# Two-layer transformer kernel: blank rows written earlier, a new order in the dense expert stage, and gate products moved from VectorE to GpSimd

## The reference, cut to what matters

```python
x = ln(x + attn0(x))          # attn0 ends in its own MLP: x1 + gelu(ln(x1) @ w1) @ w2
logits = einsum('bld,ed->ble', x, gate_weight)
kth_val = sort(logits.reshape(-1))[T * 6 - 1]        # one global threshold
gates = logits * (logits >= kth_val)
h = gelu(einsum('bld,ehd->bleh', x, w1) + b1)        # 8 experts, hidden 512
y = einsum('bleh,edh->blde', h, w2) + b2
x = ln(x + einsum('blde,ble->bld', y, gates))
x = ln(x + attn1(x)); x = ln(x + top2_moe(x))        # layer 1
```

## Time and profile before

| | |
|---|---|
| median of 3 runs | 1162.04 us (1162.0 to 1164.67) |
| profiled execution | 1153.58 us |
| its span | 1151.9 us |
| attention_0 | about 0 to 248 us |
| dense_0 | about 248 to 742 us |
| layer 1 | the rest |
| PE, DVE, ACT, POOL busy | 962.3, 863.6, 741.1, 406.5 us |
| granted TensorE clock, mean | 0.922 |

### The profile page before, as it was taken

One profiled execution on the slowest core, in us unless ns is written; L12 is line 12 of the kernel. 1 busy time (PEld: TensorE's weight loads), 2 busy tenths in 40 slices (PEclk: granted clock), 3 DMA queues, 4 the chain that ended last, 5 costly groups with the idle time before them and its releaser, 6 DMA issues. The chain is left out here.

```text
span 1151.9 us, 29135 instructions
## 1 busy us (share of the span) xinstructions
PE 962.3 (84%) x10214; PEld 611.6 (53%) x10214; DVE 863.6 (75%) x2339; ACT 741.1 (64%) x1409; POOL 406.5 (35%) x572
## 2 busy tenths in 40 slices
PE   3999999946788999949889999589888861899995
PEld 2788887733444444414334444256565541689852
DVE  2899898836569999549899877558999864688833
ACT  2666666637688888828676788346555530688834
POOL 3455455434443000000100100113676677366643
PEclk9999999978799999979999999769989875899998
DMA  4000000010002999863222110100111101233244
GB/s 128 4 3 3 4 3 3 4 58 0 1 19 74 174 170 166 163 164 97 75 86 87 55 49 17 57 22 28 32 47 48 46 23 48 77 88 83 76 108 131
DMA packets 87997, 72.61 MB, mean 63 GB/s; under 512 B 8994, under 2 KB 73764, under 8 KB 87856
## 3 DMA queue, kind: packets, MB, share of 16 engines
q1 hardware_dynamic: 79088, 60.05, 23.1%
q0 software_dynamic: 4544, 8.60, 2.3%
q10 hardware_dynamic: 4224, 2.10, 0.7%
HBM read 40.14 MB, written 31.49 MB: 62 GB/s over the span
## 5 line engine op out<-in xcount | busy, mean ns | idle before, releaser
L778 ACT ACTIVATE d__hf<-d__HB,d__d 128x512 f32<-128x512 f32 x288 | 185.8, 681 | 76.2 <-PE d__HB L1001 72.1
L839 DVE TENSOR_TENSOR d__hl<-d__hf,d__hh 128x1024 f16<-128x1024 f32 x144 | 175.6, 1224 | 30.8 <-ACT d__hh L783 28.7
L783 ACT ACTIVATE d__hh<-d__hf 128x1024 f16<-128x1024 f32 x144 | 152.2, 1057 | 4.6
L751 POOL TENSOR_SCALAR d__rstd<-d__mv 128x4 f32<-128x4 f32 x16 | 15.0, 937 | 383.8 <-DVE d__mv L953 383.8
L999 PE MATMUL d__YB<-d__hh,d__w2h 128*128 128x512 f16 x288 | 110.3, 383 | 30.7 <-DVE d__hl L839 30.7
L999 PE MATMUL d__HB<-d__xh,d__w1h 128*128 128x512 f16 x288 | 114.2, 396 | 0.0
L1000 PE MATMUL d__HB<-d__xl,d__w1h 128*128 128x512 f16 x288 | 114.1, 396 | 0.0
L1001 PE MATMUL d__HB<-d__xh,d__w1l 128*128 128x512 f16 x288 | 113.1, 393 | 0.0
L1001 PE MATMUL d__YB<-d__hh,d__w2l 128*128 128x512 f16 x288 | 110.4, 383 | 0.0
L1000 PE MATMUL d__YB<-d__hl,d__w2h 128*128 128x512 f16 x288 | 110.3, 383 | 0.0
L298 POOL TENSOR_SCALAR_AFFINE_SELECT a__pt<-a__pt 128x512 f32<-128x512 f32 x128 | 81.6, 661 | 71.7 <-ACT a__pt L341 71.5
(11 more groups left out here) (376 smaller groups left out, 2532.9 us busy)
## 6 DMA issues: line engine op xcount, KB each, us to landing
rows<-d__blank SPq DMA_DIRECT2D x72, 268.0 KB, 7.6
d__G<-gates SPq DMA_DIRECT2D x64, 256.0 KB, 3.1
c__xin<-rows SPq DMA_DIRECT2D x39, 134.0 KB, 2.2
d__stage<-e_w SPq DMA_DIRECT2D x16, 256.0 KB, 3.2
b__stage<-e_w SPq DMA_DIRECT2D x32, 128.0 KB, 2.2
c__yb<-parts SPq DMA_DIRECT2D x8, 256.0 KB, 8.3
c__yb<-parts ACTq DMA_DIRECT2D x8, 256.0 KB, 8.8
out<-c__xo SPq DMA_DIRECT2D x8, 256.0 KB, 2.3
```

The lines of the kernel that those rows point to most:

```text
L778: act.activation(hf[:, q, f], HB[:, f], gelu, scale=1.0 / WS, bias=b1[:, at:at + 1]).then_inc(s_["h_free"], 1)
L783: act.activation(hh[:, q, f - 1:f + 1], hf[:, q, f - 1:f + 1], ACT.Copy).then_inc(s_["hi_done"], 1)
L839: dve.tensor_tensor(hl[:, q, f], hf[:, q, f], hh[:, q, f], ALU.subtract).then_inc(s_["lo%d_done" % i], 1)
```

## The change

- The 72 blank DMAs move from `dense_0` to `attention_0`'s SP queue, behind its loads, five at a time, each five behind a further `hn_done` of attention's 16 steps. GpSimd fills the source, now four rows wide (128x536), once at the start; SP waits for the last of them at the stage's end.
- In `dense_0` DVE's loop over s is written in a new order: `hn` of chunk s+3 stands at the head of a step (ahead of `low(s, 1)`), the statistics of chunk s+4 stand ahead of `xa`, and the first weight split and `b2s` come later.
- The 22 raw results are folded at steps 31, 32, 34, 36, 38, 40, 41, 43, ... 68 (9 steps for 5), not one per step up to 52. `acc` has 8 chunks, not 4. The chunks end at steps 41, 44, 49, 57, 59, 65, 69 and 73.
- A raw result is multiplied by its gate row by GpSimd, in place; DVE only adds it (or copies it, where it opens a chunk). A `G` buffer is given back by the engine that used it.

The core of the diff, without declarations:

```diff
@@ attention_0, SP @@
+            sp.wait_ge(blank_set, 1)
+            for i in range(BLANKS * NC_):
+                if i % 5 == 0:
+                    sp.wait_ge(hn_done, i // 5 + 1)
+                sp.dma_start(blanks[:, i], blank[:]).then_inc(blanked, 16)
+            sp.wait_ge(blanked, 16 * BLANKS * NC_)
@@ raw_pair @@
-    i = s - FOLD_0
-    return M_JOBS + i if i >= 0 and kept_raw(M_JOBS + i) else None
+    for j in range(M_JOBS, FOLD_0):
+        if kept_raw(j) and FOLD_0 + (j - M_JOBS) * 9 // 5 == s:
+            return j
+    return None
@@ dense_0, SP @@
-            for i in range(BLANKS * NC_):
-                if i % 4 == 0:
-                    sp.wait_ge(s_["counted"], min(i // 4 + 1, ROUNDS + 2))
-                sp.dma_start(blanks[:, i], blank[:].to_broadcast([P, 4, ROW])).then_inc(s_["blanked"], 16)
...
-                wait(sp, s_["g_used"], k - G_RING + 1)
+                wait(sp, s_["g_out%d" % (k % G_RING)], k // G_RING)
@@ dense_0, GpSimd, after the rstd work of step s @@
+                if raw_pair(s) is not None:
+                    j = raw_pair(s)
+                    k = place[j]
+                    pool.wait_ge(s_["g_in%d" % (k % G_RING)], 16 * (k // G_RING + 1))
+                    pool.wait_ge(s_["yf%d" % (j % 2)], j // 2 + 1)
+                    pool.tensor_tensor(raw(j), raw(j), G[:, k % G_RING], ALU.mult).then_inc(s_["gated"], 1)
+                    pool.wait_ge(s_["gated"], j - M_JOBS + 1)
+                    pool.sem_inc(s_["g_out%d" % (k % G_RING)], 1)
@@ dense_0, fold @@
                 if kept_raw(j):
-                    ins = dve.tensor_tensor(to, raw(j), G[:, k % G_RING], ALU.mult)
+                    dve.wait_ge(s_["gated"], j - M_JOBS + 1)
+                    part = raw(j)
+                    if j in opens:
+                        sums.link(dve.tensor_copy(to, part))
...
                 if j not in opens:
-                    ins = dve.tensor_tensor(acc[:, c % 4], acc[:, c % 4], tmp[:], ALU.add)
+                    ins = dve.tensor_tensor(acc[:, c], acc[:, c], part, ALU.add)
```

More of the change, by code:

```diff
@@ L169, in parts_0, with attention_0 @@
                     step(what, s - stage, k)
-def attention_0(nc, d, keep):
+def attention_0(nc, d, keep, rows):
     with ExitStack() as ctx:
@@ L184, in attention_0 @@
         bo = m.sb("bo", [P, P])
+        blank = m.sb("blank", [P, 4, ROW])
+        blanks = rows.rearrange("(i p r) c -> p i r c", p=P, r=4)
+        blank_set, blanked = m.sem("blank_set"), m.sem("blanked")
         x = m.sb("x", [P, NT, C])
@@ L277, in _ @@
             pool.wait_ge(cleared, 4)
+            pool.memset(blank[:], BLANK).then_inc(blank_set, 1)
             pool.wait_ge(loaded, 16 * LOADS)
@@ L923, in _ @@
                         dve.wait_ge(s_["pb_free"], left[("logits", c)] + 1)
+                c = s + 3
+                if 0 <= c < M_JOBS:
+                    if c:
+                        right_full(dve, "lift", c - 1)
+                    dve.wait_ge(s_["rstd0_done"], c + 1)
+                    for a in range(4):
+                        ins = dve.tensor_scalar(hn[:, a, :], x1[:, 4 * c + a, :], mv0[:, a, 0:1], rstd0[:, a:a + 1],
+                                                ALU.subtract, ALU.mult)
+                        ins.then_inc(s_["hn_done"], 1) if a == 3 else first.inc(ins)
                 if 0 <= s < JOBS:
@@ L943, in _ @@
                     left_full(dve, *post)
+                    wait(dve, s_["xn_done"], closed)
                     res = xs if post[0] == "post" else xa
@@ L956, in _ @@
                     low(s + 1, 0)
-                if post:
-                    closed += 1
-                    dve.wait_ge(s_["rstd_done"], closed)
-                    for a in range(4):
-                        ins = dve.tensor_scalar(xa[:, 4 * c + a, :], r[:, a, :], mv[:, a, 0:1], rstd[:, a:a + 1],
-                                                ALU.subtract, ALU.mult)
-                        ins.then_inc(s_["xn_done"], 1) if a == 3 else norms.inc(ins)
-                c = s + 3
-                if 0 <= c < M_JOBS:
-                    if c:
-                        right_full(dve, "lift", c - 1)
-                    dve.wait_ge(s_["rstd0_done"], c + 1)
-                    for a in range(4):
-                        ins = dve.tensor_scalar(hn[:, a, :], x1[:, 4 * c + a, :], mv0[:, a, 0:1], rstd0[:, a:a + 1],
-                                                ALU.subtract, ALU.mult)
-                        ins.then_inc(s_["hn_done"], 1) if a == 3 else first.inc(ins)
                 c = s + 4
@@ L981, in _ @@
                         ins.then_inc(s_["var0_done"], 1) if a == 3 else first.inc(ins)
-                if s == BEGIN or 0 <= s - 5 < E:
-                    j = 0 if s == BEGIN else s - 4
+                if post:
+                    c = post[1]
+                    closed += 1
+                    dve.wait_ge(s_["rstd_done"], closed)
+                    for a in range(4):
+                        ins = dve.tensor_scalar(xa[:, 4 * c + a, :], r[:, a, :], mv[:, a, 0:1], rstd[:, a:a + 1],
+                                                ALU.subtract, ALU.mult)
+                        ins.then_inc(s_["xn_done"], 1) if a == 3 else norms.inc(ins)
+                if s == BEGIN + 1 or 0 <= s - 5 < E:
+                    j = 0 if s == BEGIN + 1 else s - 4
                     e = (j + E) % (E + 1)
```

39 lines of the change are left out of this document (16 added, 23 removed).

## The result

The changed kernel takes 1133.28 us (median of 4 runs, 1130.34 to 1134.62), the kernel before 1162.3 on the same chip; the ratio is 0.9757 [0.9723, 0.9791], or 2.4% faster. I had forecast 1120. The profiled execution took 1132.32 us with a span of 1130.6, where before it was 1153.58 and 1151.9. So the two traces differ by 21.3 us and the timed medians by 29. The traces can explain the 21.3, for which my terms said 41.7. The other 7.7 us of the timed 29 lie outside what the two traces show, so it is in part luck that the time came this near to 1120.

What follows compares the result with a forecast made beforehand. Bounds: DVE's 21.80 us wait for gates behind blank DMAs, an engine ring in m steps, TensorE in pair steps, DVE in raw fold steps. -20.7 - 16 - 5 = -41.7 us from median 1162.04 gives 1120 us; 8-in-10 range 1107 to 1134.

Steps and rivals of the forecast that it cites:

- Term 1: Dense stage: gates no longer queue behind the blank DMAs, so DVE's wait for G goes; -20.7 us, attention at 0.
- later than 248: Attention's end: ending later than 248 was named as a sign that the forecast is wrong.
- Term 2: M steps and dense start: new DVE order ends the ring through PE; -16 us, ends -21 and -6.
- The five steps: M steps: 9.8 us each with one GpSimd collision per step, 49 us in all for 60.55 before; -11.6.
- Term 3: Fold: products leave DVE and adds are spread, with some loss at eposts; -5 us.
- upper bound: Fold: each of 22 products holds DVE up for its whole 1.3 us; 227.7 for 223.0, 5 us worse.
- starts a waiting product: Fold eposts: a GpSimd product released by `rstd` meets `xa`, which takes 1.94 and not 1.11 us, 0.83 more.
- (b): Rival, fold: products cost DVE more than thought, +5 in place of -5; 1130 us, chance 0.06.
- (c): Rival, fold: products are free and the fold gains 10.6 us; 1115 us, chance 0.10.
- (a): Rival, m steps: only half the gain, -7 us, as PE waits mid-step for `low(s, 1)`; 1129 us, chance 0.18.
- (d): Rival, dense stage: the gates' way is slow of itself, so half the wait for G stays; 1130 us, chance 0.04.
- (e): Rival, fold: GpSimd's products hold the shared path 2.73 us each and DVE waits; slower, 1183 us, chance 0.02.

Runs made afterwards that it cites:

- r1_blanks_only: The kernel before with only the 72 blank DMAs, their source and the wait for them moved to attention; 1176.97 us, ratio 0.9704 to before.
- r8_no_products: The changed kernel without the 22 gate products, raw results added ungated; 1148.81 us (one run).
- r4_paced_products: The changed kernel with GpSimd's products ahead of `rstd` in its queue, each waiting for the same step's `low(s, 1)`; 1154.89 us, ratio 0.9507 to before.
- r6_after: The changed kernel, unedited, measured again beside the kernel before; 1171.65 us, ratio 0.9811 to before.

## Why the prediction was off

**Term 1, the blanks (-20.7): right.** -20.6 in the trace, and 5.2 us from `low(31, 1)` to `low(32, 1)`. r1_blanks_only has it by itself. Attention came to +2.2 in this pair of traces, just outside my -1 to +2, and it ended later than 248, which I had named as a sign of being wrong. The traces don't lay it to the blanks: without them in attention `dense_0` starts at 248.4 and 250.8, with them at 246.6 to 252.1.

**Term 2, the m steps (-16): nearly right.** It came to -14.3 from the start of `dense_0` to `low(31, 1)`. The five steps that I had put at 49 us took 48.1, but partly by luck: they were 11.03, 10.03, 10.03, 8.35 and 8.70 us and not 9.8 each. Those of 10.03 are longer because `hn` met two subtractions and not one (2.73 us for 1.11); the short ones have no further chunk to norm. At the start, for which I had -4, the first `hn` comes 4.1 us earlier in the stage (3.02 us behind its start for 7.11) and the first product 3.5 (10.48 for 14.00). DVE's timeline, in place of the earlier trace rows, shows what still holds the start: `hn` waits 0.90 to 1.59 us for each `rstd`, and two of these three `hn` take about 1.9 us for 1.11.

```profile
253.58 1.11 DVE L939 TENSOR_SCALAR d__hn<-dense__x,d__mv,d__rstd 128x128 f32<-128x128 f32 x4 [1.54 <-POOL d__rstd L764]
...
258.16 1.85 DVE L939 TENSOR_SCALAR d__hn<-dense__x,d__mv,d__rstd 128x128 f32<-128x128 f32 x4 [0.90 <-POOL d__rstd L764]
...
262.91 1.89 DVE L939 TENSOR_SCALAR d__hn<-dense__x,d__mv,d__rstd 128x128 f32<-128x128 f32 x4 [1.59 <-POOL d__rstd L764]
```

**Term 3, the fold (-5): the step that failed.** It came to +13.0, beyond the upper bound of +5 too. Three pieces of it held: the product takes 1.27 us for the 1.3 that I took, plain steps average 5.18 us, and one product at `xa` costs about what I had priced (2.06 for 1.11 us at step 57, 0.95 for my 0.83). What failed is "starts a waiting product at the very moment when DVE starts `xa`", that is, one of them. GpSimd's queue had two waiting or more at five of the eposts, since after's order puts 5 products into 9 steps behind a wait for DVE's epost; `xa` cost 1.94 us more there. The steps with the first six eposts took 10.90, 10.13, 10.97, 9.20, 10.84 and 10.98 us; without products (r8_no_products) they took 8.97, 8.20, 9.02, 8.24, 8.92 and 9.01, 10.7 us less, and at 0.83 each they would have stayed under 9.9; paced they took 8.96, 8.20, 9.02, 8.25, 9.32 and 9.02. The rest of the 22.0 us lies in the steps behind them. There I had priced PE's wait at its own length only. Behind four of these waits the clock was at the lower level, for 38 matmuls in all, and PE's busy time is 8.3 us above the paced kernel's. The upper bound fell with it: it let each product block DVE for its length once, but had no term for a TensorE that is slower afterwards. With the products paced, the part came to 215.7, which is -7.3 for my -5.

In the terms of the rivals it was (b), the products cost DVE more, to which I had given a chance of 0.06, with a price of +13 where I had written +5. (c), free products, would have given -9.0 (r8_no_products: 214.0) for my -10.6. (a), (d) and (e) did not happen. The sum of the forecast with +13 in place of -5 is -23.7, against -21.3 in the traces.

By the Trainium skill, "SBUF — State Buffer", section "Who interferes with whom", the shared port pair is an exclusive lock, a VectorE operation with at most one SBUF input outside the two-port modes stays off it, and issue order decides who blocks. The runs agree: the product that began beside the read of `YB` left it at 0.75 us (r4_paced_products, 517.91) and took 1.27 itself, while the products that began with `xa` made that one take 3.05. The number of SBUF inputs alone doesn't sort these rows: `xa` and `hn` read one tile of data each, beside the statistics of the tokens, and are held up all the same; what mode they ran in, no trace shows. I had weighed this rule by the number of products; it should have been weighed by the moments at which the queue lets them start.

## What to carry to other kernels

Work that is moved to an idle engine starts when that engine's queue lets it, not when its data are there: look for the wait ahead of it, count how many pieces pile up behind that wait, and see what the other engine does at the moment of release. Where two engines share a path, tie each piece to an event after which the other engine reads from elsewhere; here one wait and a place further ahead in the queue were worth 20 us, where the 22 products themselves cost some 2 to 3. A new wait of TensorE can cost more than its length, where a stretch at the lower clock follows it. And check whether a change moves the mark from which its parts are measured: `low(1, 1)` hid what two of the kernels here gained.

## What had not been expected of the hardware

- A wait of TensorE of 2.49 us (before the row at 551.89) was followed, from the third matmul on, by eight that started every 0.43 us and not 0.22. In the fold part of after four waits had such a sequel (2.49, 3.90, 5.43 and 3.90 us), which makes the 8.3 us of PE time. But a wait of 2.94 us had none (the row below; the next matmul starts 0.22 us later), nor had one of 2.61 in r4_paced_products. In r6_after the wait of 2.94 us in the same place had one, and the one of 2.27 us in place of the 2.49 had none. So the length of a wait alone did not decide it; what did is not shown.

```profile
533.26 0.39 PE L1013 MATMUL d__YB<-d__hh,d__w2h 128*128 128x512 f16 x1 [2.94 <-DVE d__hl L849]
```

- A tiny GpSimd instruction is held up as well. The first half of `rstd`, 128x4, took 0.96 us at 526.20, beside `low` with both inputs in SBUF, and ended about when `low` did; the same operation at 305.52 took 0.19 us.
- The source of the blanks with four rows side by side makes fewer packets for the same bytes: 60349 in the whole kernel, as this line of the page of after has it, for 87997 on the page of before.

```profile
DMA packets 60349, 72.61 MB, mean 64 GB/s; under 512 B 8994, under 2 KB 36900, under 8 KB 60208
```

- The kernel before took 1162.3, 1175.47, 1193.37 and 1211.1 us at four times, and the second and the fourth of these were on the same chip. In its second trace, 1212.0 us long, the dense parts were within 2 us of the first and 54 us of the difference lay behind `low(71, 1)`, 53 of them in the last part, the routed experts (223.1 us for 170.0): there the first trace has 1584 matmuls in 150 us at a granted clock of 1.00 (990 to 1140), the second 1498 in 195 us at 0.91 (1005 to 1200). The part behind `low(71, 1)` took 457 to 475 us in the four kernels of the first group and 417 to 419 in the four of the third, so the chip alone is not the cause. It stays open.
